# The order in which the third pair's y is kept, how its halves are joined, and where squares are added

## The reference

```python
x_hwwh = jnp.stack([x_flat, x_wh], axis=1)           # rows order, column order
xs = jnp.concatenate([x_hwwh, jnp.flip(x_hwwh, axis=-1)], axis=1)   # 4 directions, 192 channels
...
delta = jax.nn.softplus(dts + dt_bias[None, :, :, None])
def step(h, inp):                                    # 16 states per channel
    u_t, d_t, b_t, c_t = inp
    dA = jnp.exp(d_t[..., None] * A)
    h = dA * h + (d_t * u_t)[..., None] * b_t[:, :, None, :]
    y = jnp.einsum('bkdn,bkn->bkd', h, c_t)
...
y = out_y[:, 0] + inv_y[:, 0] + wh_y + invwh_y       # back to row order, summed
y = layer_norm(y, on_g, on_b)                        # over 192 channels
y = y * jax.nn.silu(z)
return jnp.einsum('bhwd,cd->bhwc', y, out_proj_w)    # 192 -> 96
```

## Time and profile before

| | us |
|---|---|
| median of 3 runs | 14108.62 (14105.9 to 14116.86) |
| profiled execution | 14119.62 |
| its span | 14117.9 |
| VectorE busy | 11941.0 (85%) |
| TensorE busy | 11123.5 (79%) |
| GpSimd busy | 9997.0 (71%) |
| ACT busy | 7061.8 (50%) |

### The profile page before, as it was taken

One profiled execution on the slowest core, in us unless ns is written; L12 is line 12 of the kernel. 1 busy time (PEld: TensorE's weight loads), 2 busy tenths in 40 slices (PEclk: granted clock), 3 DMA queues, 4 the chain that ended last, 5 costly groups with the idle time before them and its releaser, 6 DMA issues. The chain is left out here.

```text
span 14117.9 us, 98670 instructions
## 1 busy us (share of the span) xinstructions
PE 11123.5 (79%) x25456; PEld 4289.1 (30%) x25456; DVE 11941.0 (85%) x8481; ACT 7061.8 (50%) x10426; POOL 9997.0 (71%) x4365
## 2 busy tenths in 40 slices
PE   7877878778787787777877778777787877878777
PEld 2333323333233332323323233233332333233332
DVE  6999579995799957999579995799957999579995
ACT  4454454554545554455545455454554545445454
POOL 3999239992499924999249992499924999249991
PEclk9899889998899988999889998899988899888998
DMA  4677336773367734677346773467734677247772
GB/s 125 214 220 214 83 115 214 221 213 81 120 214 220 215 77 121 214 220 214 77 122 214 218 215 75 124 214 218 216 73 127 215 220 215 69 128 216 219 216 67
DMA packets 693758, 2391.62 MB, mean 169 GB/s; under 512 B 137088, under 2 KB 137088, under 8 KB 683264
## 3 DMA queue, kind: packets, MB, share of 16 engines
q1 hardware_dynamic: 693152, 2384.91, 57.6%
HBM read 2300.09 MB, written 67.11 MB: 168 GB/s over the span
## 5 line engine op out<-in xcount | busy, mean ns | idle before, releaser
L1076 POOL TENSOR_TENSOR state<-state,c_sb 128x1024 f32<-128x1024 f32 x3072 | 7177.9, 2357 | 451.1 <-ACT carry L903 448.7
L839 PE MATMUL ps<-state,wt 128*128 128x512 f32 x12288 | 6360.8, 660 | 142.3 <-ACT ya L897 106.7
L839 PEld LDWEIGHTS ps<-state,wt 128*128 128x128 f32 x12288 | 2559.5, 212 | 3044.0 <-issue 2481.1
L1035 DVE TENSOR_TENSOR_SCAN state<-decay,carry,ps 128x1024 f32<-128x1024 f32 x1440 | 3379.4, 2347 | 87.0 <-DVE ps L1022 37.4
L1065 POOL TENSOR_TENSOR dbu<-b_sb,du 128x1024 f32<-128x1024 f32 x1152 | 2715.8, 2357 | 897.6 <-DVE du L1050 897.6
L903 ACT COPY carry<-state 128x1 f32<-128x1 f32 x3072 | 585.7, 191 | 4870.3 <-DVE state L1035 4860.6
L816 PE MATMUL ps<-parts,sel 114*128 114x512 bf16 (+1 forms) x3840 | 1279.9, 418 | 2080.6 <-DVE state L1035 2078.9
L1022 DVE TENSOR_TENSOR ps<-ps,du 128x1024 f32<-128x1024 f32 x1920 | 2323.7, 1210 | 0.8
L945 ACT ACTIVATE decay<-delta,a_neg 128x1024 f32<-128x1024 f32 x1920 | 2194.9, 1144 | 6.3
L1035 DVE TENSOR_TENSOR_SCAN state<-ps,carry,dbu 128x1024 f32<-128x1024 f32 x864 | 2013.4, 2330 | 4.0 <-POOL dbu L1065 4.0
L816 PEld LDWEIGHTS ps<-parts,sel 114*128 114x128 bf16 (+1 forms) x3840 | 260.3, 100 | 3636.8 <-DVE state L1035 3356.6
(11 more groups left out here) (189 smaller groups left out, 10728.2 us busy)
## 6 DMA issues: line engine op xcount, KB each, us to landing
c_sb<-bc SPq DMA_DIRECT2D x2048, 512.0 KB, 4.3
c_sb<-bc SPq DMA_DIRECT2D x2048, 256.0 KB, 5.5
b_sb<-bc SPq DMA_DIRECT2D x768, 512.0 KB, 4.7
b_sb<-bc SPq DMA_DIRECT2D x768, 256.0 KB, 5.4
x_nat<-x SPq DMA_DIRECT2D x17, 1536.0 KB, 9.1
gates<-gate_a SPq DMA_DIRECT2D x8, 2048.0 KB, 6.4
gate_a<-gates SPq DMA_DIRECT2D x8, 2048.0 KB, 8.9
x_tok<-x SPq DMA_DIRECT2D x288, 48.0 KB, 1.8
```

The lines of the kernel that those rows point to most:

```text
L839: mm = pe.matmul(py[:, q * CH:(q + 1) * CH], col("ident"), state[:, slot(g, n), q * CH:(q + 1) * CH], start=(n == 0), stop=False)
L1035: dve.tensor_tensor_scan(state[:, slot(g, n), way], rate, what, 0.0 if fresh else carry[:, n:n + 1], ALU.mult, ALU.add)\
L1076: pool.tensor_tensor(state[:, slot(g, n), :], state[:, slot(g, n), :], c_sb[:, n % CRING, :], ALU.mult).then_inc(S["weighted"], 1)
```

## The change

In the scan, `take_y` for T = 2 and 5 writes the halves by two copies, partitions 0 to 63 as before and partitions 64 to 127 turned, so that all of `yr` is in row order. `add_y` for T = 5 must then read the two halves in different orders: it uses two products with the matrices `halves`, each of which has one half of the identity and zeros.

In `post_a`, the fold is one product with `fold_w` (two identities side by side and on top of each other: both halves summed, in all 128 output rows). The mean is taken from `yr` itself right behind it, not from `yrc`. GpSimd adds the squares of the 64 channels (`sqr`) onto partitions 0 to 63 of `sqa`, and the variance is one product. The affine step of ACT goes into VectorE's `on_unit` (scale) and `gate` (bias). The lags shrink by one turn. In the set-up VectorE builds the two matrices.

```diff
+    fold_w = put("fold_w", [128, 128], F32)
+    halves = put("halves", [128, 2, 128], F32)
...
+                low, up = col("ident")[:, 0:DR], col("ident")[:, DR:128]
+                nc.vector.tensor_tensor(fold_w[:, 0:DR], low, up, ALU.add)
+                nc.vector.tensor_tensor(fold_w[:, DR:128], low, up, ALU.add)
+                nc.vector.memset(halves[DR:128, 0, :], 0.0)
+                nc.vector.memset(halves[0:DR, 1, :], 0.0)
+                for i in range(2):
+                    nc.vector.tensor_copy(halves[DR * i:DR * i + DR, i, :], col("ident")[DR * i:DR * i + DR, :])
...
-                        old = (ua, None, ur, ya, None, yr)[T]
+                        old = (ua, None, ur, ya, None, None)[T]
                         for q in range(2):
                             o = py[:, q * CH:(q + 1) * CH]
-                            if T % 3 == 1:
+                            if T == 5:
+                                by_col = yr[:, :].rearrange("p (h w) -> p w h", w=W)[:, rows(2 * at + q), :]
+                                pe.matmul(o, halves[:, 0, :], yr[:, sl(2 * at + q)], start=False, stop=False)
+                                mm = pe.matmul(rc(o), halves[:, 1, :], by_col, start=False, stop=True)
+                            elif T % 3 == 1:
                                 by_col = ya[:, :].rearrange("p (h w) -> p w h", w=W)[:, rows(2 * at + q), :]
                                 mm = pe.matmul(rc(o), col("ident"), by_col, start=False, stop=True)
...
-                        act.copy(chunk(yr if T % 3 == 2 else ya, T, at), like(py[:, :], T)).then_inc(S["y_taken"], 1)
+                        if T % 3 == 2:
+                            by_col = yr[DR:128, :].rearrange("p (h w) -> p w h", w=W)
+                            act.copy(yr[0:DR, span(at * SC, SC)], py[0:DR, :])
+                            last = act.copy(by_col[:, span(at * (SC // H), SC // H), :],
+                                            py[DR:128, :].rearrange("p (w h) -> p w h", h=H))
+                        else:
+                            last = act.copy(chunk(ya, T, at), like(py[:, :], T))
+                        last.then_inc(S["y_taken"], 1)
...
-                    first = cols["ident"][0] + DR
-                    hi_ = wt[:, first:first + 128]
-
                     def fold(j):
 
-                        turned = yr[:, :].rearrange("p (w h) -> p h w", h=H)[:, rows(j), :]
-                        wait_free(pe, S["yr_copied"], j)
-                        pe.matmul(bank["yr"], col("ident"), yr[:, sl(j)], start=True, stop=False)
-                        pe.matmul(rc(bank["yr"]), hi_, turned, start=False, stop=True).then_inc(S["yr_mm"], 1)
-
-                    def sum_192(j, a, r, name, ready, freed, done):
-
-                        pe.wait_ge(ready, j + 1)
-                        wait_free(pe, freed, j)
-                        pe.matmul(bank[name], col("ones_di"), a[:, sl(j)], start=True, stop=False)
-                        pe.matmul(bank[name], col("ones_di", DR), r[:, sl(j)],
-                                  start=False, stop=True).then_inc(done, 1)
+                        wait_free(pe, S["on_centered"], j)
+                        pe.matmul(bank["yr"], fold_w[:, :], yr[:, sl(j)], start=True, stop=True)\
+                          .then_inc(S["yr_mm"], 1)
+                        pe.matmul(bank["on_mean"], col("ones_di"), ya[:, sl(j)], start=True, stop=False)
+                        pe.matmul(bank["on_mean"], col("ones_di"), yr[:, sl(j)], start=False, stop=True)\
+                          .then_inc(S["on_mean_mm"], 1)
+
+                    def var_192(j):
+
+                        pe.wait_ge(S["sq_added"], j + 1)
+                        wait_free(pe, S["on_log"], j)
+                        pe.matmul(bank["on_var"], col("ones_di"), sqa[:, sl(j)], start=True, stop=True)\
+                          .then_inc(S["on_var_mm"], 1)
...
                     staggered((0, fold),
-                              (1, lambda j: sum_192(j, ya, yrc, "on_mean", S["yr_copied"], S["on_centered"],
-                                                    S["on_mean_mm"])),
-                              (2, lambda j: sum_192(j, sqa, sqr, "on_var", S["on_squared"], S["on_log"],
-                                                    S["on_var_mm"])),
-                              (4, out_proj),
-                              (5, lambda j: ln_sum(pe, j, x1, S["x1_ready"], bank["ln2_mean"], S["ln2_centered"],
+                              (1, var_192),
+                              (3, out_proj),
+                              (4, lambda j: ln_sum(pe, j, x1, S["x1_ready"], bank["ln2_mean"], S["ln2_centered"],
                                                    S["ln2_mean_mm"])),
-                              (6, lambda j: ln_sum(pe, j, sq2, S["ln2_squared"], bank["ln2_var"], S["ln2_log"],
+                              (5, lambda j: ln_sum(pe, j, sq2, S["ln2_squared"], bank["ln2_var"], S["ln2_log"],
                                                    S["ln2_var_mm"])))
...
-                    def on_affine(j):
-                        act.wait_ge(S["on_unit"], j + 1)
-                        act.activation(ya[:, sl(j)], ya[:, sl(j)], ACT.Identity, bias=col("on")[:, 0, 1:2],
-                                       scale=col("on")[:, 0, 0:1])
-                        act.activation(yrc[:, sl(j)], yrc[:, sl(j)], ACT.Identity, bias=col("on", DR)[:, 1, 1:2],
-                                       scale=col("on", DR)[:, 1, 0:1]).then_inc(S["on_affine"], 1)
-
...
-                    staggered((0, yr_copy), (1, on_square),
-                              (2, lambda j: ln_root(act, j, bank["on_var"], S["on_var_mm"], rs, S["on_log"],
+                    staggered((0, yr_copy), (0, on_square),
+                              (1, lambda j: ln_root(act, j, bank["on_var"], S["on_var_mm"], rs, S["on_log"],
                                                     S["on_rsqrt"], 128)),
-                              (3, on_affine),
-                              (5, lambda j: ln_square(act, j, cen2, S["ln2_centered"], sq2, S["ln2_squared"])),
-                              (6, lambda j: ln_root(act, j, bank["ln2_var"], S["ln2_var_mm"], rs2, S["ln2_log"],
+                              (4, lambda j: ln_square(act, j, cen2, S["ln2_centered"], sq2, S["ln2_squared"])),
+                              (5, lambda j: ln_root(act, j, bank["ln2_var"], S["ln2_var_mm"], rs2, S["ln2_log"],
                                                     S["ln2_rsqrt"])),
-                              (7, ln2_affine))
+                              (6, ln2_affine))
...
+                    for j in range(NCH):
+                        pool.wait_ge(S["on_squared"], j + 1)
+                        pool.tensor_tensor(sqa[0:DR, sl(j)], sqa[0:DR, sl(j)], sqr[:, sl(j)], ALU.add)\
+                            .then_inc(S["sq_added"], 1)
...
                         dve.tensor_tensor(ya[:, sl(j)], ya[:, sl(j)], bank["on_mean"], ALU.subtract)
+                        dve.wait_ge(S["yr_copied"], j + 1)
                         dve.tensor_tensor(yrc[:, sl(j)], yrc[:, sl(j)], bank["on_mean"][0:DR, :], ALU.subtract)\
                            .then_inc(S["on_centered"], 1)
...
                         dve.wait_ge(S["on_rsqrt"], j + 1)
-                        dve.tensor_tensor(ya[:, sl(j)], ya[:, sl(j)], rs[:, sl(j)], ALU.mult)
-                        dve.tensor_tensor(yrc[:, sl(j)], yrc[:, sl(j)], rs[0:DR, sl(j)], ALU.mult)\
-                           .then_inc(S["on_unit"], 1)
+                        dve.scalar_tensor_tensor(ya[:, sl(j)], ya[:, sl(j)], col("on")[:, 0, 0:1], rs[:, sl(j)],
+                                                 ALU.mult, ALU.mult).then_inc(S["on_unit"], 1)
+                        dve.scalar_tensor_tensor(yrc[:, sl(j)], yrc[:, sl(j)], col("on", DR)[:, 1, 0:1],
+                                                 rs[0:DR, sl(j)], ALU.mult, ALU.mult).then_inc(S["on_unit"], 1)
 
                     def gate(j):
                         if j == 0:
                             dve.wait_ge(S["back_in"], 48)
-                        dve.wait_ge(S["on_affine"], j + 1)
-                        dve.tensor_tensor(ya[:, sl(j)], ya[:, sl(j)], gate_a2[:, sl(j)], ALU.mult)
-                        dve.tensor_tensor(yrc[:, sl(j)], yrc[:, sl(j)], gate_r2[:, sl(j)], ALU.mult)\
-                           .then_inc(S["gated"], 1)
+                        dve.wait_ge(S["on_unit"], 2 * j + 1)
+                        dve.scalar_tensor_tensor(ya[:, sl(j)], ya[:, sl(j)], col("on")[:, 0, 1:2], gate_a2[:, sl(j)],
+                                                 ALU.add, ALU.mult)
+                        dve.wait_ge(S["on_unit"], 2 * j + 2)
+                        dve.scalar_tensor_tensor(yrc[:, sl(j)], yrc[:, sl(j)], col("on", DR)[:, 1, 1:2],
+                                                 gate_r2[:, sl(j)], ALU.add, ALU.mult).then_inc(S["gated"], 1)
...
```

(8 more changed lines are left out.)

## The result

| | before | changed |
|---|---|---|
| median of 6 runs, us | 14116.5 (14105.9 to 14126.6) | 14167.6 (14165.8 to 14177.1) |
| profiled execution, us | 14119.6 | 14177.1 |
| its span, us | 14117.9 | 14175.2 |

The ratio is 1.0036, with a 95% interval of 1.0026 to 1.0047: the change makes the kernel 51 us slower. I had forecast 14179 (14137 to 14220) and slower; on the median of all six runs of before the same +70 us would be 14187.

The account below looks back on a forecast made before the run. VectorE was taken to bound the scan and TensorE post_a. Scan loss 18.1 less post_a gain 9.5 is 8.6 us an image slower, x 8 = 69, plus 1 for set-up: +70 us, 14179 us (14137 to 14220).

Parts of the forecast that it names:

- What bounds the kernel: In the scan VectorE, busy 1323 of 1394 us, makes up no lateness later; in post_a TensorE, 112 of 128.
- The copies: Scan, take_y for T = 2 and 5: pair holds ACT 2.63 us, not 0.91; VectorE stalls 1.66 us a chunk.
- the faster rival: Scan: a copy of half the lanes costs half, pair 1.32 us; 14093, or 14056 with warm fill; chance 0.06.
- The products of T = 5: Scan, add_y: four products in place of two last 5.3 us, 0.4 us unhidden, so a stall of 2.09 us.
- for three chunks: Scan, T = 5: a stall of 2.09 us in each of three chunks, 6.3 us an image.
- The end of the scan: Last T = 5 chunk, uncovered: 3.42 us for the sum and 1.82 for the copies, 5.2 us together.
- The turn: post_a, one slice: 7.7 us in place of 10.59, set by a loop through four engines, not TensorE's 7.3.
- The fill: post_a's first turns: TensorE at half clock after pauses; variance of slice 2 at 28.3 to 30.3 us.
- The drain: post_a, variance of slice 7 to last x1_ready: 13.7 us in place of 16.6, out_proj 3.8 of it.
- Net: Per image: 18.1 us lost in the scan less 9.5 gained in post_a, 8.6 us slower.
- The rival with a warm TensorE: TensorE stays warm in post_a's fill and drain: gain 14.2 us, net 3.9 us an image slower, 14141; chance 0.16.
- The rival that GpSimd waits for VectorE: post_a: VectorE's L412 (0.67 us) delays the GpSimd sum by its whole length; turn 8.3 us, 14210; chance 0.06.

Follow-up runs that it names:

- e8_no_pool_sum: The changed kernel without GpSimd's sum of squares, the variance again two products, of sqa and of sqr: 14198.3 us, 31 above the changed kernel.
- e3_one_product: The changed kernel with add_y of T = 5 again one contiguous product a half chunk, the two copies kept: 14139.4 us, 28 below the changed kernel.
- e4_one_later: The changed kernel with softplus_one moved from step n = 5 to n = 6: 14120.5 us, 47 below the changed kernel.
- e9_unit_first: The changed kernel with on_unit of a slice put ahead of skip in VectorE's queue: 14216.0 us, 48 above the changed kernel.
- e5_before_one_later: The kernel before with softplus_one alone moved from step n = 5 to n = 6: 14093.0 us, 27 below before (0.9981).

## Why the prediction was right, and where its sizes were not

- **What bounds the kernel**: right. VectorE in the scan makes up almost nothing later: of 21.6 us of stalls and end, 20.3 reached the start of `post_a`.
- **The copies**: right in kind and place. Term "2.63 us for the pair" was 2.74, since the first copy of the pair is 1.01 us from the next start and not 0.91. The stall was 1.88 us in place of 1.66. That half the lanes cost the full price, the point that decided against the faster rival, is measured: 1.00 and 1.93 us.
- **The products of T = 5**: the 5.3 us and the 0.4 us unhidden were right (2.31 = 1.88 + 0.43). The step that failed is "for three chunks": the last chunk has no softplus, ACT has no other work at that step, and the copy waits 1.86 us for the sum, not 0.4; the chunk cost 4.1 us, not 2.1. That TensorE had room was also wrong there: 0.28 and 0.86 us of VectorE's wait are for L825 and 0.43 for the sums.
- **The end of the scan**: 5.2 us expected, 5.3 found; 1.3 us of the stalls before it was absorbed in GpSimd's last steps. Scan in all: 18.1 expected, 20.3 in the trace, 22 by the median of the run of that half alone (20 by its traced execution).
- **The turn**: 7.7 us expected, 7.59 found, with the loop and not TensorE as the limit, confirmed from the other side by `e8_no_pool_sum`.
- **The fill**: mis-sized for this kernel, with the right mechanism. I put the variance of slice 2 at 28.3 to 30.3 us; it starts at 26.7 in five images and at 27.9 in three. The low level of the clock is there (2.08 us for the call at 1540.12), but the variance of slice 1 is back at the full rate (1.19 us), and the gates' loads hide most of what is left. My range did come in the same stage of two other runs, at 29.5 (`e3_one_product`, seven images) and 28.4 (`e4_one_later`, all eight). Nothing in the rows of before tells which of them a kernel gets, so from those rows this part of the sum could not be had closer than some 3 us an image.
- **The drain**: mis-sized. I carried over the half-clock `out_proj` of before (3.8 us). In the changed kernel the pause before it is 0.45 us and not 1.87, and the call takes 1.10 us in place of 1.83. The step from the variance of slice 7 to `x1_ready` is 11.7 us in place of 13.7.
- **Net**: forecast 18.1 - 9.5 = 8.6 us an image; the first image shows 20.3 - 14.5 = 5.8, the eight images of the two traces 20.9 - 13.7 = 7.2, and 51 us are 6.4 an image. Two misses of opposite sign, 2.2 to 2.8 us more lost in the scan and 4.2 to 5 more won in `post_a`, partly cancelled; that the time fell so near the forecast is in part luck. The rival with a warm TensorE had nearly the right gain (14.2 us), although TensorE was not warm in the fill, and the scan's larger loss brought the time back between it and my forecast.
- **The rival that GpSimd waits for VectorE**: it did not happen in the steady turns, for that product (L421 in the changed kernel, 0.68 us from 1578.73) ends before GpSimd starts at 1580.07. It is real all the same (`e9_unit_first`); only the order of VectorE's queue keeps it away.

What stays open: what decides how many of the first turns run at half clock. It moved `post_a` by up to 2.9 us an image between runs with the same code in that stage, and so it also stands in the comparisons of `e3_one_product`, `e4_one_later`, `e8_no_pool_sum` and `e9_unit_first`. The stage of before has it too: in `e5_before_one_later` one of the eight took 97.6 us in place of about 91, with calls of 2.07 us from 1535.98 on. The traced executions lie 57 us apart where the medians lie 51, because the traced one is the slowest of the six of the changed kernel.

## What to carry to other kernels

A rearrangement that makes one stage cheaper must be priced at the place where the data is written, and there in the queue of the engine that writes: the eight strided copies that the kernel already had showed, to about 0.2 us, what the new ones would cost. When a stall goes, look for the wait that stood behind it: moving the work behind the copy took 0.93 us from the first wait and gave 0.43 us back at the next. And a layout needed only at the end should be made only by the last pass, into a buffer that this pass leaves free; that turned +51 us into -48. And where a stage starts with short products and pauses, look at every image of the trace, not only the first: here the same code took 76.5, 77.8 or 79.4 us.

## What the runs showed of the hardware

- An ACT copy of 64 lanes and 1024 elements takes 1.00 us, and 1.93 us with a stride of 64 elements on the output; 128 lanes take the same.
- GpSimd's sum of 64 lanes and 512 elements takes 1.26 us, beside 2.357 for 1024 elements.
- GpSimd and VectorE hold each other up where VectorE reads two operands in SBUF: 1.26 to 1.72 us for the one and 0.74 to 1.75 for the other. In the scan of before, where the rows of VectorE's scans and products have one input in PSUM, GpSimd kept its 2.357 us.
- TensorE's float32 call (two instructions of 512 columns) took 2.07 us at half clock and 1.12 at full. In the first turns of `post_a`, with pauses of 3.88 us before the variance, the number of calls at half clock differed between images of one run and between runs of the same code there; the variance of slice 2 started 26.7 to 29.5 us into the stage.
